# A four-layer Flamingo block on one core: copies moved in the self-attention stage, a norm taken into the position stage, weights awaited by set

## The reference

```
x = x + tanh(g_xattn[0]) * L0_xattn(layernorm(x), ctx, ctx)     # cross attention, 16 heads of 16
x = x + tanh(g_ffn[0])   * L0_ffn(layernorm(x))                 # expert by token position: 8 experts, 14 tokens each
x = x + tanh(g_xattn[1]) * L1_xattn(layernorm(x), ctx, ctx)
x = x + tanh(g_ffn[1])   * L1_ffn(layernorm(x))                 # routed experts with low-rank parts
x = x + tanh(g_xattn[2]) * L2_xattn(layernorm(x), ctx, masks)   # self attention, norm, cross attention, norm, feed-forward, norm
x = x + tanh(g_ffn[2])   * L2_ffn(layernorm(x))                 # product keys
x = x + tanh(g_xattn[3]) * L3_xattn(layernorm(x), ctx, masks)
x = x + tanh(g_ffn[3])   * L3_ffn(layernorm(x))                 # routed experts

layernorm(x) = (x - mean) / sqrt(var + 1e-5)                    # without gain; inside L2 with gain and shift
L0_ffn: h = silu(x w1[e]) * (x w3[e]);  out = h w2[e]
```

## Time and profile before

| what | value |
|---|---|
| median of 3 runs | 3105.9 us |
| the profiled execution | 3098.41 us, its span 3096.7 us |
| busy share of the span | PE 85%, DVE 60%, ACT 44%, POOL 34% |
| TensorE clock granted, mean | 0.912 of full |
| context stage | from 4.65 us to 309.9 us |
| tail of the position stage, norm, query stage | 668.5 to 713.9 us |
| self stage, steps 0 to 15 | 1340.75 to 1488 us |

### The profile page before, as it was taken

How to read it: one execution, slowest core, us unless ns; L and a number is a source line. 1 busy time by engine, 2 the same in 40 slices (tenths; PEclk the granted TensorE clock), 3 DMA queues, 4 the chain that set the end, 5 groups by cost and what they waited for, 6 DMA issues and landing times. The chain is left out here.

```text
span 3096.7 us, 57443 instructions
## 1 busy us (share of the span) xinstructions
PE 2617.7 (85%) x21112; PEld 2040.3 (66%) x21112; DVE 1853.1 (60%) x3909; ACT 1353.8 (44%) x2664; POOL 1044.5 (34%) x1259
## 2 busy tenths in 40 slices
PE   7998699987988999868599897877867994999995
PEld 7998377874776666446277664554545873888884
DVE  4555687137854333366388436778658864677675
ACT  3444466225662111345456433344334661555552
POOL 2343200002012222256412232553242113677772
PEclk9999699997998999988689999988987995999998
DMA  7888664345630000251556300000036633455553
GB/s 218 244 246 244 179 164 137 134 124 149 182 122 5 1 1 1 77 134 37 136 147 168 117 0 1 1 1 1 1 97 158 178 91 123 186 210 190 188 200 104
DMA packets 153095, 363.52 MB, mean 117 GB/s; under 512 B 26496, under 2 KB 110336, under 8 KB 137136
## 3 DMA queue, kind: packets, MB, share of 16 engines
q1 hardware_dynamic: 141120, 275.13, 31.6%
q0 software_dynamic: 11760, 85.51, 7.8%
HBM read 271.43 MB, written 88.67 MB: 116 GB/s over the span
## 5 line engine op out<-in xcount | busy, mean ns | idle before, releaser
L1026 ACT ACTIVATE arena<-ps 125x448 f32<-125x448 f32 x768 | 404.2, 544 | 314.6 <-PE ps L935 311.0
L1059 DVE TENSOR_REDUCE arena<-ps 112x2 f32<-112x750 f32 x384 | 348.3, 930 | 76.7 <-PE ps L919 71.2
L469 POOL TENSOR_SCALAR ln_var<-ln_mv 112x1 f32<-112x1 f32 x144 | 35.0, 243 | 820.3 <-DVE ln_mv L463 817.9
L919 PE MATMUL ps<-wreg,arena 96*112 96x375 bf16 x768 | 218.6, 374 | 82.2 <-DMA arena<-query_parts 51.8
L2696 PE MATMUL ps<-moe_x_r,moe_w_r 128*128 128x256 f32 x2016 | 255.6, 287 | 18.3 <-DVE arena L2848 16.8
L2696 PEld LDWEIGHTS ps<-moe_x_r,moe_w_r 128*128 128x128 f32 x2016 | 247.3, 193 | 23.7 <-DVE arena L2848 20.3
L935 PEld LDWEIGHTS ps<-arena,wreg 98*125 98x125 bf16 x2304 | 215.6, 142 | 60.7 <-issue 18.7
L935 PE MATMUL ps<-arena,wreg 98*125 98x112 bf16 x2304 | 237.0, 228 | 3.2 <-ACT arena L1026 3.0
L945 PE MATMUL ps<-arena 125*17 125x112 f32 x6144 | 199.8, 263 | 0.6 <-ACT arena L1026 0.6
L2262 POOL TENSOR_TENSOR arena<-arena 112x1024 f32<-112x1024 f32 x64 | 121.0, 1904 | 198.1 <-DVE arena L2385 155.1
L2848 DVE SCALAR_TENSOR_TENSOR arena<-arena 128x256 f32<-128x256 f32 x168 | 141.0, 848 | 60.7 <-ACT arena L2743 59.7
(11 more groups left out here) (337 smaller groups left out, 5773.5 us busy)
## 6 DMA issues: line engine op xcount, KB each, us to landing
wreg<-key_parts SPq DMA_DIRECT2D x288, 187.5 KB, 3.9
key_parts<-arena SPq DMA_DIRECT2D x128, 281.2 KB, 3.9
arena<-query_parts SPq DMA_DIRECT2D x108, 224.0 KB, 4.7
values<-arena SPq DMA_DIRECT2D x64, 357.0 KB
arena<-values SPq DMA_DIRECT2D x64, 357.0 KB
arena<-key_parts SPq DMA_DIRECT2D x96, 187.5 KB, 3.8
query_parts<-arena SPq DMA_DIRECT2D x48, 336.0 KB, 2.5
wreg<-in_e_w SPq DMA_DIRECT2D x16, 704.0 KB, 5.4
```

Source lines behind the costliest of these rows:

```text
L919: mm = pe.matmul(ps[0:T, 2 * (p % 2) + e, 0:S2], queries(b)[0:SROWS, hd, :], keys[r][0:SROWS, hd, :], start=True, stop=True)
L1026: act.activation(probs[k % PROBS], ps[0:KN, 4 + k % 2, 0:GT], ACT.Exp, scale=scale).then_inc(at_probs, 1)
L1059: dve.tensor_reduce(negmax[r % 2][:, 2 * p:2 * p + 2], ps[0:T, 2 * (p % 2):2 * (p % 2) + 2, 0:S2], AX.X, ALU.max, negate=True).then_inc(at ...
```

## The change

Three edits that touch different stages.

In the context stage each set has a semaphore of its own, and ACT waits for the two transfers of set i just ahead of rounding set i. The four semaphores are the ones that the masked attention uses much later for its masks, so its wait values rise by 32.

In the position stage the norm of `x` is done by batch inside the stage's tail with `RowNorm`, and the `norm_stage` behind it is gone: statistics and moments stand on DVE behind each batch's addition, the deviation on POOL, `apply` and `evacuate` on ACT, and PE turns the rows of batch b-4 behind the turning back of batch b. The stage's meeting now comes behind all of that.

In the self stage ACT's `evacuate` of batch b-5 moves from part 3 of step b to part 0 of step b, ahead of `copy_turned`. POOL's `keep_scaled` is cut in two: the product stays in part 3, the sum moves to part 0 of the next step.

```diff
@@ context stage
-                    sp.dma_start(w[:, i], a["attn_w"][s, :, 1:3]).then_inc(loaded, 16)
-                    sp.dma_start(bv[:, i, :], a["attn_rows"][s, 0].partition_broadcast(128)).then_inc(loaded, 16)
+                    sp.dma_start(w[:, i], a["attn_w"][s, :, 1:3]).then_inc(kv_in[i], 16)
+                    sp.dma_start(bv[:, i, :], a["attn_rows"][s, 0].partition_broadcast(128)).then_inc(kv_in[i], 16)
...
-                act.wait_ge(loaded, weights_ready)
                 for i in range(NKV):
+                    act.wait_ge(kv_in[i], 32)
                     act.activation(w_r[0][:, i], w[:, i], ACT.Copy).then_inc(kv_w, 1)
@@ self stage, POOL
                             if k == 3 and g * GB + b >= 4:
-                                norm.keep_scaled(pool, g * GB + b - 4)
+                                norm.scale_kept(pool, g * GB + b - 4)
+                            if k == 0 and g * GB + b >= 5:
+                                norm.shift_kept(pool, g * GB + b - 5)
@@ self stage, ACT
+                            if k == 0 and b >= 5:
+                                norm.evacuate(act, b - 5, turned)
                             if k == 1 and b >= 4:
                                 norm.apply(act, b - 4)
-                            if k == 3 and b >= 5:
-                                norm.evacuate(act, b - 5, turned)
                             if k == 0 and has(b, -2):
                                 out.copy_turned(act, o0 + b - 2, u)
@@ position stage
+            norm = RowNorm(x, **norm)
+            slots = [ps[:, 6 + u, 0:DC * T] for u in range(2)]
+            LAG = 4
...
                     mm.then_inc(e0_turned, 1)
+                    if b >= LAG:
+                        norm.turn(pe, b - LAG, slots[b % 2], 2)
+                for b in range(B - LAG, B):
+                    norm.turn(pe, b, slots[b % 2], 2)
...
                 experts(act, step)
+                for b in range(B + 1):
+                    if b < B:
+                        norm.apply(act, b)
+                    if b > 0:
+                        norm.evacuate(act, b - 1, slots[(b - 1) % 2])
+
+            def gpsimd(pool):
+                for b in range(B):
+                    norm.deviation(pool, b)
...
                                              ALU.mult, ALU.add).then_inc(ffn_added, 1)
+                    if b > 0:
+                        norm.moments(dve, b - 1)
+                    norm.stats(dve, b, ffn_added, b + 1)
+                norm.moments(dve, B - 1)
...
-            position_experts_stage(4, weights)
-
-            norm_stage(x, 1e-5)
+            position_experts_stage(4, weights, dict(eps=1e-5))
```

More of the change, by code:

```diff
@@ L241, in build @@
         kv_w, kv_high, kv_lo = sem("kv_w"), sem("kv_high"), sem("kv_lo")
-        kv_v = sem("kv_v")
+        kv_v, kv_in = sem("kv_v"), [sem(f"kv_in_or_mask{i}") for i in range(len(KV_SET))]
         part_made, part_hi, part_res, part_mid, part_lo = sem("part_made"), sem("part_hi"), sem("part_res"), sem("part_mid"), sem("part_lo")
@@ L250, in context_stage @@
             NKV = len(KV_SET)
-            weights_ready = expect(2 * NKV)
             ones_made = expect_made(4)
@@ L486, in keep_scaled, with scale_kept, shift_kept @@
             def keep_scaled(self, pool, b):
-                kept = self.before("kept", b)
+                self.scale_kept(pool, b)
+                self.shift_kept(pool, b)
+            def scale_kept(self, pool, b):
                 pool.wait_ge(ln_normed, self.before("normed", b) + 1)
-                at_least(pool, ln_kept, kept - XN + 1)
+                at_least(pool, ln_kept, self.before("kept", b) - XN + 1)
                 pool.tensor_tensor(ln_scale[:, b % XN, :], self.rows(b), ln_gain[0:T, 0, :], ALU.mult).then_inc(ln_scaled, 1)
+            def shift_kept(self, pool, b):
                 pool.wait_ge(ln_scaled, self.before("scaled", b) + 1)
@@ L774, in build @@
         at_scores, at_probs, at_pv = sem("at_scores"), sem("at_probs"), sem("at_pv")
-        at_mask, at_pen0, at_pen = [sem(f"at_mask{r}") for r in range(RING)], sem("at_pen0"), sem("at_pen")
+        at_mask, at_pen0, at_pen = kv_in, sem("at_pen0"), sem("at_pen")
         at_count = {"call": 0, "mask": 0}
@@ L1078, in penalty @@
                 def penalty(b, r, turn):
-                    dve.wait_ge(at_mask[r], (turn - turn0 + 1) * 32)
+                    dve.wait_ge(at_mask[r], 32 + (turn - turn0 + 1) * 32)
                     at_least(dve, at_pv, (n0 + b - 3) * STEPS)
@@ L1199, in step @@
                             if k == 3 and g * GB + b >= 4:
-                                norm.keep_scaled(pool, g * GB + b - 4)
+                                norm.scale_kept(pool, g * GB + b - 4)
+                            if k == 0 and g * GB + b >= 5:
+                                norm.shift_kept(pool, g * GB + b - 5)
                 over_groups(pool, step)
+                norm.shift_kept(pool, B - 5)
                 for b in range(B - 3, B):
@@ L1429, in load_ahead, with position_experts_stage @@
                 self.load(sp, 0, 0)
-        def position_experts_stage(gate, weights):
+        def position_experts_stage(gate, weights, norm):
             arena.clear()
@@ L1525, in vector @@
                                              ALU.mult, ALU.add).then_inc(ffn_added, 1)
-            stage(sync, None, scalar, vector, tensor)
+                    if b > 0:
+                        norm.moments(dve, b - 1)
+                    norm.stats(dve, b, ffn_added, b + 1)
+                norm.moments(dve, B - 1)
+            stage(sync, gpsimd, scalar, vector, tensor)
         rt_logits, rt_step, rt_exp = sem("rt_logits"), sem("rt_step"), sem("rt_exp")
```

## The result

| | before | after |
|---|---|---|
| median (3 runs each) | 3105.9 us | 3075.08 us (3072.57 to 3077.55) |
| ratio to before | | 0.9891, interval 0.9872 to 0.9910 |
| profiled execution, its span | 3098.41, 3096.7 us | 3072.57, 3070.7 us |
| TensorE clock granted, mean | 0.912 | 0.917 |

What follows compares the result with a forecast made beforehand. It gave each stage its own limit, PE in the context stage. Self -24.5, context -7.0 and position +8.5 sum to -23.0: 3098.4 becomes 3075.4, plus 7.5 for the median of runs, 3082.9 us; range 3073 to 3098.

Steps and rivals of the forecast that it cites:

- PE is the bound of the stage: Context stage: PE, busy 98.5 of 100 us, sets its length, so an earlier PE start ends it 7.0 us earlier.
- the self term: Self stage: moving the copies removes PE's wait and the lower clock behind it, gaining 24.5 us over 11 steps.
- Position term: Position stage: query loads issued 16.3 us later behind POOL's deviations, query stage 7.8 shorter; a loss of 8.5 us.
- the 29.1: Query stage behind the position stage: time from SP's first load to the next memset, taken from layer 3, 29.1 us.
- Rival 2: Position stage: the tail follows DVE, costing only +3.4; total -28.1, time 3078; chance 0.10.
- the 7.8 that I charged: Self stage: forecast length of a step, 7.7 plus 0.1 charged for fitting the copies elsewhere, in place of 10.03 us.
- the eleventh step of my sum: Self stage: the gain of 10.03 - 7.8 per step was counted for 11 steps, 24.5 us in all.
- Rival 1: Self stage: the clock stays low, so the gain is only 12.9; total -11.4, time 3094.5; chance 0.15.
- rivals 3 and 4: Self stage: the wait only moves, total +1.5, chance 0.08; or the moved copies delay ACT's work, total +10.0, chance 0.05.
- Context term: Context stage: ACT rounds the first set at 11.5 in place of 18.5, so the stage ends 7.0 us earlier.
- The lower end of 3.4: Context stage: if ACT's queue behind the last set is late, DVE's low parts decide and the gain is 3.4 us.
- The range: Whole kernel: 3073 (self gain 26.7, cheap position tail) to 3098 us (clock stays low, context gain at its lower end).

Runs made afterwards that it cites:

- the last of the self series: The changed kernel with ACT's two copies in part 3 of a step, behind its exponential but ahead of its copy; ratio 0.9977 to the kernel before.

## Why the prediction was right and wrong

The change was larger than forecast. Two steps of the prediction failed. "PE is the bound of the stage" was wrong as a mechanism: with two buffers, the round from ACT to the landing of the store paced the context stage (16.75 us per batch in place of 17.60 to 18.38 once there were four). And the self term, right in its mechanism, was mis-sized: 24.5 where the traces show 29.0. The second (4.5), 4.0 of drift in unchanged stages and an offset of 5.0 between single execution and median put the time below the forecast; the first, 5.75 the other way in the pair of traces, hid part of it.

**Position term (+8.5): right**, in sum (+8.3 and +8.4) and in parts: POOL's pitch, the first deviation 1.6 us behind the first addition, the longer tail, the wait for the query weights (7.55). The price was measured alone. Taking the late loads away gave 4.5, taking POOL's row away (with the lag changed too) 2.2; the clock of 0.74 in place of 0.99 at the start of the query products is a third difference that the sum held only inside the 29.1. Rival 2, a tail that follows DVE for +3.4, is refuted.

**Self term (-24.5): right in its cause, 4 to 5 us too small.** The step is 7.645, not the 7.8 that I charged for fear of the new place: 10 x 0.155 = 1.55. From the start of step 15 to the next stage's load it takes 27.56 before and 22.90 after, 4.66 less, and the eleventh step of my sum held only 2.2 of that: 2.4 more lie in the tail that I had left out. The last 0.5 lies ahead of step 0. The division of a step: against the kernel before, PE's wait for the turn gives 1.72, products at the higher clock 8.30 - 7.09 = 1.21, and 0.55 comes back as waiting for the exponentials: 2.38. That the lower clock follows from the wait is seen in every kernel of the series (0.85 with 1.72 of wait per step, 0.87 with 1.45, 1.00 without), but a wait with the full clock was never made, so the two weren't tried apart. Rival 1 is refuted, and rivals 3 and 4 with it: the copies cost nothing in parts 0 and 2, and in part 3 ahead of the exponential. The prediction called itself wrong if idle time turned up before the transposes of the exponentials. It did, 5.5 us in ten steps, but steps 2 to 4 had the same 0.56 per step, which the sum of the step held: the sign was badly chosen.

**Context term (-7.0): the step that failed is "PE is the bound of the stage, so the stage ends earlier by as much as PE starts earlier".** PE had its 7.2 us at the third set and 1.6 at the end. The stage goes round ACT, DVE, POOL, store and landing with two buffers; ACT's wait for landings stood in the trace of before, and I took a busy share of 98.5% for a bound without asking why ACT waited 41 us for `key_parts` in the same 100 us. Four buffers showed it (718 products in place of 690), and with them PE's lead is kept (4.99 and 4.99). The lower end of 3.4, for the case that "the queue behind ACT's wait for the last set is late after all", describes what happened in the first batch (ACT's first key part 3.55 earlier), though I had DVE's low parts decide there, and the trace has ACT's rounding. Its size was -1.25, -5.2 and -8.2 in three comparisons of traces and -7.5 between medians, so the number 7.0 is not refuted by the time; what holds in all of them is a lead of 3.6 to 5.3 behind batch 0, which is my lower end's mechanism, and a pace set by landings. In the pair shown the term was too large by 5.75.

**The offset.** I set the profiled execution of before (3098.4) against the median of before (3105.9) and added 7.5; after's median lies 2.5 above its own profile. Those 5.0 us are most of the error of 7.8, the other 2.8 is the sum (23.0 predicted, 25.8 in the traces). In the sum, the context term's error of 5.75 was covered by self (4.5), by drift in unchanged stages (4.0) and by position (0.2): that the sum came near is partly luck. The profiled execution of before is not one of the three behind its median, that of after is. What made the former 7.5 us shorter than the median stays open, since the three have no trace. A difference of that size between traces is at hand in one place: the context stage ends at 309.90 in it and at 319.64 to 321.83 in three later traces with the old wait.

**The range** began at 3073. The median of after lies in it, but the ratio of 0.9891 applied to 3105.9 gives 3072.0, just below. Its end had the self term at 26.7, which was an end only because the tail behind the last step was left out.

## What to carry to other kernels

- Before an engine is called the bound of a stage, look who else waits there: a busy PE that has 4% fewer instructions per 100 us than it can do can be paced by the loop behind it. Two more buffers gave 15 to 22 us, by the trace compared with, where the earlier start gave 1 to 8.
- A copy that frees a buffer belongs ahead of an instruction that waits for another engine, not behind it; the three places ahead that were tried here were as good as each other.
- Moving a norm inside a stage is no gain if its small instructions form the longest row and the next stage's loads come behind it.
- A difference of two single traces has a spread; read the same stretch in every trace at hand.

## What the runs showed of the hardware

- The landing of a key store took a median of 3.9 us in three traces (before, after, and the last of the self series) and 4.1 to 4.2 in the nine others with two buffers, and the pace went with it: 17.59 to 17.75 us per batch in the three, 18.13 to 18.38 in the others. The medians of before in these groups are 3105.9 and 3102.9 against 3112.9 to 3120.1. With four buffers landings took 5.1 to 5.3 us and the pace was 16.75 to 16.85 in all four such kernels.
- A wait of PE of 1.55 us was followed by products that took up to twice as long for some 3 us, the granted clock being 0.54 in the first 2 of them. In the first two steps of the self stage the same code takes 7.65 and 6.54, or 8.86 and about 7.8 us, from one trace to the other: 2.5 us that no edit made.
